# A selective-scan stage that reads its state out four tokens at a time, from channels that are neighbours in DRAM

## The chip, the cores and the metric

One core of one Trainium2 chip runs the whole program. The metric is device microseconds of one execution: the median of three executions for the kernel before, and one more execution with the hardware profiler, whose trace is read below. TensorE is called PE in the rows, its weight loads PEld, VectorE DVE, ScalarE ACT, GpSimd POOL, SyncE SP.

## The reference, cut to what matters

The program is a stack of eight blocks on 2048 tokens of 128 features (8 sequences of 256 tokens). The change touches one of them, a bidirectional Mamba block: two selective scans, m = 1 over each sequence and m = 2 over the reversed one, with 256 channels (E) and 64 states (N) a channel.

```
def step(h, inp):
    xt, dtt, Bt, Ct = inp
    dA = jnp.exp(dtt[:, :, None] * A)
    h = dA * h + (dtt * xt)[:, :, None] * Bt[:, None, :]
    y = jnp.einsum('ben,bn->be', h, Ct)
    return (h, y)
...
y = ys.transpose(1, 0, 2) + xc * Dp
y = y * _silu(z)
```

For every token the state h (256 channels x 64 states) is decayed, a term is added, and it is contracted with the 64 values of C of that token.

## The kernel before, in words

`mamba_scan` runs once for m = 1 and once for m = 2. A partition holds one state of one half of the channels: 64 states x 2 halves (g = 0, 1) = 128 partitions. The free axis holds 4 channels x 256 tokens. One **iteration** handles these 4 channels of each half for one sequence; 32 iterations (`NS`, 4 units u of 8 iterations i) make one sequence, tb; 8 sequences make one scan stage. So each stage has 256 iterations, and both stages 512. A sequence is one turn of a hardware loop on PE, ACT, DVE and POOL (the first is written out before the loop); SP's program is written out in full.

An iteration n goes through five queues, each in its own order:

- SP loads dt * x of the 4 channels, the same for all 64 states: two DMAs (`load_dtx`, one for each half of 64 partitions, 256 KB each) into one of 4 buffers `kept` (they lie in the memories `residual` and `norm`). It waits until POOL has finished product n - 4. `load_rows` brings the step sizes dt as bf16 rows, for PE.
- POOL multiplies with B (`times_b`, L3550) into one of 4 buffers `dBx`; it waits for the load of n and for scan n - 4.
- PE spreads dt over the 64 states (`cast`, L3436, two products, banks 0 and 1). Each half waits until ACT has read that bank in iteration n - 1.
- ACT takes the exponential (`exps`, L3492, four instructions) into one of 2 PSUM buffers `decay`; it waits for scan n - 2.
- DVE runs the recurrence as one scan instruction over 1024 elements (L3572) into `h`, which has 2 halves of 32 channels, one for each unit in turn.

The contraction with C comes after: `chunk` on PE (L3449), 9 iterations behind the cast. C stands on the weight side. `c_spread` holds, for each token, a tile of 16 columns that is zero but for the two columns (one for each half g) of that token, so 8 tokens that follow one another can be accumulated into 16 rows of PSUM. Four such groups of tokens go to PSUM partitions 0, 32, 64 and 96. A chunk covers 32 tokens of the 32 channels of a unit with 32 products of 16 columns by 32 channels. Each product stands in the trace as two PE records and two PEld records, as every f32 product does. At the end of a unit ACT copies the bank to `y_tokens` (`move`, L3511). Once a sequence, in iteration 11 of the next, `by_features` multiplies with the diagonal D (L3456) and turns `y_tokens` back with the identity (L3460), DVE multiplies with the gate (`gate`). At the start of a sequence ACT fills `c_spread` from C (`build`, L3504); its zeros come from DRAM by one DMA at the start of each stage (L3417).

Of the kernel before, what the change touches and what calls it, by code (L numbers as in the profile page):

```python
# [13 lines left out]
BF16 = mybir.dt.bfloat16  # L14
# [5 lines left out]
P = 128  # L20
# [2907 lines left out]
def lay_out_mamba(i, d, np):  # L2928
# [19 lines left out]
    d["l3a_zero"] = np.zeros(T * 16, np.float32)  # L2948
# [414 lines left out]
def mamba_scan(k, m, mem):  # L3363
# [5 lines left out]
    TALL = 16  # L3369
# [3 lines left out]
    with Part(k) as p:  # L3373
        h = p.sb("h", [P, 2, SJ, T])
        spread = p.sb("c_spread", [P, T, TALL])
        extra = p.sb("dBx", [P, 2, SSTEP])
        rows = p.sb("dt_rows", [SROWS, 2, 2, T], BF16)
        ysb = p.sb("y_tokens", [P, NI, P])
# [13 lines left out]
        state = lambda n, x: (2 * n + x // 2) * 8 + x % 2  # L3392
        by_token = lambda g: k.bank[YBANK].rearrange("p (n g s) -> p n g s", g=SE, s=8)[:, :, g, :]
        in_eights = lambda a: a.rearrange("p (n s) -> p n s", s=8)

        def tokens(tb, lo=0, n=T):
            return bass.ds(tb * T + lo, n)

        with nc.Block() as block:
            @block.sync  # L3400
            def _(sp):
                def load_rows(u):
                    tb, jb = u // SUNITS, u % SUNITS
                    sp.wait_ge(q["cast"], 2 * NI * u + 2 * NI)
                    sp.dma_start(rows[:, u % 2], mem["dt_rows"][:, 2 * jb:2 * jb + 2, tb * T:(tb + 1) * T]).then_inc(rows_in[u % 2], 16)

                def load_dtx(n):
                    tb, jb, i = n // NS, n // NI % SUNITS, n % NI
# [8 lines left out]
                sp.dma_start(spread[:].rearrange("p t c -> p (t c)"), k.dram["l3a_zero"].partition_broadcast(P)).then_inc(q["spread_zeroed"], 16)  # L3417
# [9 lines left out]
            def _(pe):  # L3427
                def cast(tb, l):
                    n, u, i = tb * NS + l, l // NI, l % NI
                    if i == 0:  # L3430
                        pe.wait_ge(rows_in[u % 2], 16 * (tb * (SUNITS // 2) + u // 2 + 1))
                    for x in range(2):
                        pe.wait_ge(q["decayed"], 2 * n + x + 1)
                        out = k.bank[x].rearrange("p (j t) -> p j t", t=T)[:, :, 1:]
                        a = 2 * i + x
# [272 lines left out]
```

## Time and profile before

| | |
|---|---|
| median of three executions | 5022.83 us (5010.32 to 5029.96) |
| profiled execution | 5026.35 us |
| its span, first to last instruction | 5024.5 us |
| granted TensorE clock, mean over the span | 0.831 |
| PE busy in the span | 3553.1 us (71%) |
| DVE busy | 3276.9 us (65%) |
| POOL busy | 2511.8 us (50%) |
| ACT busy | 2346.7 us (47%) |
| the two scan stages, first to last scan | about 3029 to 3902 us and 4042 to 4902 us |

A scan stage is found by the lines L3572 and L3550. Rows of idle time name what ended it: `issue` means that the engine waited for nothing that the profile shows. `PEclk` is the granted TensorE clock as a share of 2.4 GHz.

### The profile page before, as it was taken

The numbers are of one execution on the slowest core, as the hardware profiler recorded it, in microseconds if no ns is written. First come the engines' busy times: TensorE is split into PE (matmuls) and PEld (weight loads), VectorE is DVE, ScalarE is ACT, GpSimd is POOL, SyncE is SP. The second block draws the span as 40 slices with busy tenths as digits, with TensorE's granted clock in tenths as the row PEclk, the third lists the DMA queues.
The fourth block names the chain that finished last, engine by engine and source line by source line (L and its number), as shares of the span: only waits on it lengthen the run. The fifth ranks groups of instructions, "written<-read, shape, count | busy, mean of one in ns | idle before, by whom it ended". The sixth has DMA issues, their size and how long they took to land. (4 is left out here: it accounts for less than half of the span.)

```text
span 5024.5 us, 130170 instructions
## 1 busy us (share of the span) xinstructions
PE 3553.1 (71%) x50301; PEld 2406.5 (48%) x50301; DVE 3276.9 (65%) x5840; ACT 2346.7 (47%) x5437; POOL 2511.8 (50%) x2256
## 2 busy tenths in 40 slices
PE   5888888888488688688899744565656545556564
PEld 3666666666366466474477412333333323333333
DVE  5777777776476576562388666566667556666675
ACT  3555555555244344233366554444445444444451
POOL 2555555555343342430133426666667066666772
PEclk8999999999777778788999866777778867777787
DMA  1000000000000000000000028767777187776860
GB/s 49 8 9 9 9 9 9 9 8 8 15 0 6 13 0 6 5 0 24 17 1 0 14 78 184 154 154 165 153 161 163 47 183 159 158 155 156 164 159 31
DMA packets 263394, 333.14 MB, mean 66 GB/s; under 512 B 97056, under 2 KB 127024, under 8 KB 260912
## 3 DMA queue, kind: packets, MB, share of 16 engines
q1 hardware_dynamic: 262832, 325.11, 29.2%
q8 instruction: 418, 6.85, 0.6%
q14 instruction: 144, 1.18, 0.1%
HBM read 306.12 MB, written 18.87 MB: 65 GB/s over the span
## 5 line engine op out<-in xcount | busy, mean ns | idle before, releaser
L3492 ACT ACTIVATE banks<-banks,alog 128x255 f32<-128x255 f32 x2048 | 787.8, 447 | 864.2 <-PE banks L3436 796.8
L3449 PE MATMUL banks<-h,c_spread 128*16 128x32 f32 x32768 | 614.6, 234 | 550.0 <-issue 543.7
L3449 PEld LDWEIGHTS banks<-h,c_spread 128*16 128x16 f32 x32768 | 493.1, 115 | 856.1 <-issue 829.9
L3572 DVE TENSOR_TENSOR_SCAN h<-banks,dBx 128x1024 f32<-128x1024 f32 x256 | 576.0, 2279 | 392.5 <-ACT banks L3492 328.7
L3550 POOL TENSOR_TENSOR dBx<-residual,b_by_state 128x1024 f32<-128x1024 f32 x256 | 601.3, 2362 | 356.4 <-DVE h L3572 293.0
L3572 DVE TENSOR_TENSOR_SCAN h<-banks,norm_featmajor 128x1024 f32<-128x1024 f32 x256 | 576.4, 2277 | 226.2 <-ACT banks L3492 213.8
L3550 POOL TENSOR_TENSOR norm_featmajor<-norm,b_by_state 128x1024 f32<-128x1024 f32 x256 | 601.7, 2361 | 215.5 <-DVE h L3572 161.3
L3436 PE MATMUL banks<-dt_rows,selectors 96*128 96x510 bf16 x1024 | 446.7, 506 | 280.7 <-issue 126.3
L3436 PEld LDWEIGHTS banks<-dt_rows,selectors 96*128 96x128 bf16 x1024 | 87.3, 103 | 392.9 <-issue 212.8
L973 POOL TENSOR_TENSOR weighted<-probs,f 128x1024 f32<-128x1024 f32 x64 | 120.7, 1902 | 215.5 <-DVE f L1024 214.3
L2611 POOL TENSOR_TENSOR out_factors<-out_norms,exponents 128x4 f32<-128x4 f32 x64 | 64.4, 1007 | 288.9 <-DVE out_norms L2776 288.9
L2667 DVE SCALAR_TENSOR_TENSOR qk<-banks,taps,qk 128x255 f32<-128x255 f32 (+2 forms) x384 | 167.2, 477 | 26.6 <-ACT qk L2405 15.1
L2667 DVE SCALAR_TENSOR_TENSOR v_featmajor<-banks,taps,v_featmajor 128x255 f32<-128x255 f32 (+2 forms) x384 | 167.2, 477 | 24.4 <-ACT v_featmajor L2405 13.8
L1766 POOL TENSOR_TENSOR squares<-qkv_ahead 128x1024 f32<-128x1024 f32 x32 | 60.9, 1903 | 197.4 <-ACT qkv_ahead L1702 197.4
L2587 POOL TENSOR_TENSOR blocks_inv<-blocks_inv,block_products 64x14 f32<-64x14 f32 (+6 forms) x448 | 117.1, 261 | 63.8 <-issue 0.3
L2585 POOL TENSOR_TENSOR block_products<-blocks_inv,blocks 64x14 f32<-64x14 f32 (+6 forms) x448 | 114.0, 254 | 67.1 <-issue 5.5
L1595 PE MATMUL banks<-wqkv,x_batch 128*128 128x512 f32 x192 | 120.7, 779 | 26.9 <-DVEq L1792 23.8
L1211 POOL TENSOR_TENSOR norms<-norms,minus_half 128x64 f32<-128x64 f32 x8 | 84.7, 10592 | 106.0 <-DVE norms L1242 106.0
L159 POOL MEMSET minus_half<- 128x4 f32 x7 | 0.7, 102 | 270.3 <-POOLq L365 162.9
L255 PE MATMUL banks<-ident,norm 128*128 128x128 f32 x112 | 31.2, 435 | 135.9 <-ACT norm L230 134.1
L2475 ACT ACTIVATE v<-banks,beta_k 128x128 f32<-128x128 f32 x256 | 73.0, 368 | 100.0 <-PE banks L2255 100.0
L2405 ACT ACTIVATE qk<-banks,taps 128x256 f32<-128x256 f32 x128 | 53.6, 470 | 139.3 <-PE banks L2125 139.2
(451 smaller groups left out, 8768.8 us busy)
## 6 DMA issues: line engine op xcount, KB each, us to landing
residual<-mamba_dtx_rows SPq DMA_DIRECT2D x512, 256.0 KB, 5.8
norm<-mamba_dtx_rows SPq DMA_DIRECT2D x512, 256.0 KB, 6.3
dt_rows<-mamba_dt_rows SPq DMA_DIRECT2D x64, 96.0 KB, 7.0
delta_blocks<-A_turned SPq DMA_DIRECT2D x256, 8.0 KB, 1.5
inv_turned<-delta_blocks SPq DMA_DIRECT2D x256, 8.0 KB, 1.7
mamba_dtx_rows<-dtx SPq DMA_DIRECT2D x16, 256.0 KB, 2.3
c_spread<-in_l3a_zero SPq DMA_DIRECT2D x2, 2048.0 KB, 10.5
blocks<-delta_blocks SPq DMA_DIRECT2D x32, 64.0 KB, 2.1
```

Source lines behind the costliest of these rows:

```text
L973: nc.gpsimd.tensor_tensor(blocks(SW[:, u]), blocks(S[:, j % 2, u]), over(f[:, j % 2, 16 * u:16 * u + 16], T // NJ), ALU.mult).then_inc(wei ...
L1211: nc.gpsimd.tensor_tensor(nrm[:], nrm[:], half[:], ALU.pow).then_inc(norm_ready, 1)
L1595: i = nc.tensor.matmul(k.bank[4 + n][:], xb[:, t * P:(t + 1) * P], wqkv[:, n * 512:(n + 1) * 512], start=True, stop=True)
L2475: i = fn(v[:, hg, c, h, :], k.bank[c][:, h * P:(h + 1) * P], ACT.Identity, scale=sp[:, hg, c, h:h + 1])
L2585: tt(tmp[:, 0:j, 0:n], over(U[:, 0:j, j], n), across(N[:, j, j + 1:], j), ALU.mult)
L2587: i = tt(U[:, 0:j, j + 1:], U[:, 0:j, j + 1:], tmp[:, 0:j, 0:n], ALU.add)
L2667: i = stt(out=dst[:, back:], in0=k.bank[4 + n % 2][:, m * T:(m + 1) * T - back], scalar=taps[:, first + m, j:j + 1], in1=dst[:, back:], op ...
L3436: nc.tensor.matmul(out, mem["sel"][:, 2 * a:2 * a + 2, :].rearrange("r g n -> r (g n)"), rows[:, u % 2, :, 1:], start=True, stop=True).the ...
L3449: mm = nc.tensor.matmul(k.bank[OBANK][32 * c:32 * c + TALL, i * SJ:(i + 1) * SJ], spread[:, t, :], h[:, u % 2, :, t], start=s == 0, stop=s ...
L3492: e = fn(per_step(decay[l % 2])[:, 2 * x + j, 1:], k.bank[x][:, j * T + 1:(j + 1) * T], ACT.Exp, scale=mem["A"][:, at:at + 1])
L3550: nc.gpsimd.tensor_tensor(per_step(dBx[l % 4]), per_step(kept[l % 4]), across(mem["B"][:, tokens(tb)], 4), ALU.mult).then_inc(q["dbx"], 1)
L3572: v.tensor_tensor_scan(flat(h[:, u % 2, 4 * i:4 * i + 4, :]), decay[l % 2], dBx[l % 4], 0.0, ALU.mult, ALU.add).then_inc(q["scanned"], 1)
```

## The change

- **Four tokens in one product.** `c_spread` now has tiles of 32 columns for 4 tokens that follow one another (4 groups of 4 tokens, 2 halves). One product takes the states of those 4 tokens for all 32 channels as 128 moving columns. It computes every pair of the 4 tokens, and only the pairs with equal tokens are used. A chunk has 8 products of 32 by 128 in place of 32 of 16 by 32, and a unit's result fills all 512 columns of the bank in place of 256.
- **What follows from it.** `move` copies 512 columns in place of 256, and `y_tokens` is four times as large in its last axis; `by_features` turns it back with 16 products of 32 columns in place of 8 of 64. The zeros are 9280 bytes for a partition in place of 16384.
- **Neighbouring channels.** The 4 channels of an iteration were 2 + 2, 8 apart; now they are 4 in a row. A load reads one run of 4 KB for each partition in place of two of 2 KB, with the same bytes and the same two DMAs.
- **Rows of dt.** `load_rows` brings rows for two units at once (half as many DMAs, twice the size), and earlier: in iteration 4 of the 16 before, not in iteration 5 of the 8 before.

```
-    TALL = 16
+    NG, TALL, WIDE = 4, 32, 144
...
-        spread = p.sb("c_spread", [P, T, TALL])
+        spread = p.sb("c_spread", [P, NG * 4 * WIDE + 16])
-        ysb = p.sb("y_tokens", [P, NI, P])
+        ysb = p.sb("y_tokens", [P, NG, P, 4])
...
                 def load_dtx(n):
                     sp.wait_ge(q["dbx"], n + 1)
                     for g in range(SE):
-                        src = mem["dtx_rows"][tb, g].rearrange("(a r) t -> a r t", r=8)[2 * i:2 * i + 2, 2 * jb:2 * jb + 2, :]
-                        sp.dma_start(kept[n % 4][g * 64:(g + 1) * 64, :].rearrange("p (a x) -> p a x", a=2),
-                                     src.rearrange("a r t -> a (r t)").partition_broadcast(64)).then_inc(dtx_in[n % 4], 16)
+                        sp.dma_start(kept[n % 4][g * 64:(g + 1) * 64, :],
+                                     mem["dtx_rows"][tb, g, at:at + 4, :].rearrange("j t -> (j t)").partition_broadcast(64)).then_inc(dtx_in[n % 4], 16)
...
-                    if n % NI == 5 and n // NI + 1 < B * SUNITS:
-                        load_rows(n // NI + 1)
+                    if n == 2:
+                        load_rows(1)
+                    if n % (2 * NI) == 4 and 1 < n // (2 * NI) + 1 < 2 * B:
+                        load_rows(n // (2 * NI) + 1)
...
                 def chunk(tb, l):
-                    for s in range(8):
+                    part = i // 2
+                    out = k.bank[OBANK][:, part * P:(part + 1) * P].rearrange("p (j w) -> p j w", w=4)
+                    for quad in (2 * (i % 2), 2 * (i % 2) + 1):
                         for c in range(4):
-                            t = i * SJ + c * 8 + s
-                            mm = nc.tensor.matmul(k.bank[OBANK][32 * c:32 * c + TALL, i * SJ:(i + 1) * SJ], spread[:, t, :], h[:, u % 2, :, t],
-                                                  start=s == 0, stop=s == 7)
+                            t, at = part * 64 + c * 16 + quad * 4, (part * 4 + c) * WIDE + quad * TALL
+                            mm = nc.tensor.matmul(out[32 * c:32 * c + TALL], spread[:, at:at + TALL], h[:, u % 2, :, t:t + 4],
+                                                  start=quad == 0, stop=quad == 3)
...
-                    for i in range(NI):
-                        mm = nc.tensor.matmul(k.bank[YBANK][:, i * 64:(i + 1) * 64], ysb[:, i, :], used, start=False, stop=i == NI - 1)
+                    for n in range(NG):
+                        for w in range(4):
+                            mm = nc.tensor.matmul(out[:, n, :, :, :, w], ysb[:, n, :, w], ones[:, :, :, :, w], start=False,
+                                                  stop=n == NG - 1 and w == 3)
...
-                    out = ysb[:].rearrange("p n (a r) -> p n a r", r=8)[:, :, :, 2 * u:2 * u + 2]
-                    fn(out, k.bank[OBANK][:, 0:T].rearrange("p (n a r) -> p n a r", n=NI, r=2),
-                       ACT.Copy).then_inc(q["moved"], 1)
+                    out = ysb[:].rearrange("p n (x i v) w -> p n x i (v w)", x=2, i=NI)[:, :, u % 2, :, 16 * (u // 2):16 * (u // 2) + 16]
+                    fn(out, k.bank[OBANK].rearrange("p (n i v) -> p n i v", n=NG, v=16), ACT.Copy).then_inc(q["moved"], 1)
```

On PE, inside the loop over the sequences, one iteration stood like this before: two casts with the register work of their waits, then the 32 products of a chunk.

```order
L3433 ISA
L3436 MATMUL banks<-dt_rows,selectors 128x2x255
L3433 REGISTER_ALU
L3436 MATMUL banks<-dt_rows,selectors 128x2x255
L3449 MATMUL banks<-h,c_spread 16x32 x32
```

The same iteration of the changed kernel:

```order
L3434 ISA
L3436 MATMUL banks<-dt_rows,selectors 128x2x255
L3434 REGISTER_ALU
L3436 MATMUL banks<-dt_rows,selectors 128x2x255
L3451 MATMUL banks<-h,c_spread 32x128 x8
```

Nothing moved on PE; the row of 32 small products became one of 8 products with four times the columns.

On SP, iterations 8 to 29 of the first sequence before (`residual` and `norm` are the four `kept` buffers, two iterations each):

```order
L3405 DMA dt_rows<-mamba_dt_rows 96x2x256
L3412 DMA norm<-mamba_dtx_rows 64x2x512 x4
L3412 DMA residual<-mamba_dtx_rows 64x2x512 x4
L3412 DMA norm<-mamba_dtx_rows 64x2x512 x4
L3412 DMA residual<-mamba_dtx_rows 64x2x512 x4
L3405 DMA dt_rows<-mamba_dt_rows 96x2x256
```

The same queue of the changed kernel, about the load of rows that stands in iteration 20:

```order
L3410 DMA norm<-mamba_dtx_rows 64x1024 x4
L3410 DMA residual<-mamba_dtx_rows 64x1024 x2
L3404 DMA dt_rows<-mamba_dt_rows 96x4x256
L3410 DMA residual<-mamba_dtx_rows 64x1024 x2
L3410 DMA norm<-mamba_dtx_rows 64x1024 x4
```

The loads of dt * x kept their place and number, each with one run of 1024 elements in place of two of 512; the loads of rows stand half as often.

## Rows read from the trace of the kernel before

**Rows 1.** Stretches of both scan stages: length, busy us, clock, DMA share, GB/s.
```profile
core 0: us, PE busy (x) PEld busy (x) DVE busy (x) ACT busy (x) POOL busy (x), PEclk, DMA share, GB/s
3025.00:3930.00 905.00, 533.23 (x17108) 320.64 (x17109) 582.16 (x277) 416.53 (x1088) 597.21 (x255) 0.76 0.73 154
```

**Rows 2.** The scans alone (L3572), seven sequences of each stage.
```profile
3028.80:3809.40 780.60, 501.49 (x225) 0.74 0.76 160
4041.60:4813.30 771.70, 501.27 (x224) 0.75 0.76 162
```

**Rows 3.** Page, costliest groups: busy us, mean ns, idle before, releaser.
```profile
L3492 ACT ACTIVATE banks<-banks,alog 128x255 f32<-128x255 f32 x2048 | 787.8, 447 | 864.2 <-PE banks L3436 796.8
L3449 PE MATMUL banks<-h,c_spread 128*16 128x32 f32 x32768 | 614.6, 234 | 550.0 <-issue 543.7
L3572 DVE TENSOR_TENSOR_SCAN h<-banks,dBx 128x1024 f32<-128x1024 f32 x256 | 576.0, 2279 | 392.5 <-ACT banks L3492 328.7
L3550 POOL TENSOR_TENSOR dBx<-residual,b_by_state 128x1024 f32<-128x1024 f32 x256 | 601.3, 2362 | 356.4 <-DVE h L3572 293.0
```

**Rows 4.** PE in order of time, 3546 to 3588 us.
```profile
3546.87 0.51 PE L3449 MATMUL banks<-h,c_spread 128*16 128x32 f32 x23 [2.51 <-issue]
3547.32 1.03 PE L3436 MATMUL banks<-dt_rows,selectors 96*128 96x510 bf16 x2
3548.28 1.09 PE L3449 MATMUL banks<-h,c_spread 128*16 128x32 f32 x64
3549.31 1.03 PE L3436 MATMUL banks<-dt_rows,selectors 96*128 96x510 bf16 x2
3550.28 0.73 PE L3449 MATMUL banks<-h,c_spread 128*16 128x32 f32 x35
3553.51 0.63 PE L3449 MATMUL banks<-h,c_spread 128*16 128x32 f32 x29 [2.50 <-issue]
...
3586.69 1.03 PE L3436 MATMUL banks<-dt_rows,selectors 96*128 96x510 bf16 x2 [9.31 <-issue]
```

**Rows 5.** DMA packets by queue and kind, 3030 to 3930 us.
```profile
q8 instruction: 148, 2.42, 1.2%
```

**Rows 6.** DVE in order of time, the same stretch as rows 4.
```profile
3549.62 4.47 DVE L3572 TENSOR_TENSOR_SCAN h<-banks,norm_featmajor 128x1024 f32<-128x1024 f32 x2 [2.24 <-ACT banks L3492]
3589.00 2.29 DVE L3572 TENSOR_TENSOR_SCAN h<-banks,dBx 128x1024 f32<-128x1024 f32 x1 [9.38 <-ACT banks L3492]
```

**Rows 7.** POOL in order of time, start of stage m = 1, then of m = 2.
```profile
3026.60 2.34 POOL L3550 TENSOR_TENSOR dBx<-residual,b_by_state 128x1024 f32<-128x1024 f32 x1 [5.34 <-DMA residual<-mamba_dtx_rows]
...
3041.94 4.64 POOL L3550 TENSOR_TENSOR norm_featmajor<-norm,b_by_state 128x1024 f32<-128x1024 f32 x2 [2.08 <-DMA norm<-mamba_dtx_rows]
...
3063.20 2.34 POOL L3550 TENSOR_TENSOR norm_featmajor<-norm,b_by_state 128x1024 f32<-128x1024 f32 x1 [0.83 <-DMA norm<-mamba_dtx_rows]
...
4039.51 2.34 POOL L3550 TENSOR_TENSOR dBx<-residual,b_by_state 128x1024 f32<-128x1024 f32 x1 [5.40 <-DMA residual<-mamba_dtx_rows]
...
4075.72 2.34 POOL L3550 TENSOR_TENSOR dBx<-residual,b_by_state 128x1024 f32<-128x1024 f32 x1 [1.41 <-DMA residual<-mamba_dtx_rows]
```

**Rows 8.** Stretches at the starts of the stages, all engines, columns as in rows 1.
```profile
3023.00:3044.00 21.00, 9.22 (x16) 1.67 (x16) 13.30 (x6) 15.23 (x37) 13.68 (x6) 0.50 0.95 195
3044.00:3064.00 20.00, 10.61 (x311) 5.39 (x310) 17.56 (x8) 9.22 (x24) 17.43 (x9) 0.59 0.96 183
3017.00:3022.00 5.00, 0.00 (x0) 0.00 (x0) 0.00 (x0) 0.00 (x0) 2.34 (x1) 0.50 0.98 406
```

**Rows 9.** PE records of one line in a stretch, 32 columns (L3449).
```profile
3504.70:3505.90 1.20, 1.10 (x64) 0.50 0.66 148
```

**Rows 10.** The same for 128 columns (L3621), at both clocks.
```profile
3922.31:3924.31 2.00, 2.00 (x10) 0.55 0.00 0
3926.00:3931.00 5.00, 5.00 (x47) 1.00 0.00 0
```

**Rows 11.** PE in order of time at the end of stage m = 1.
```profile
3906.82 2.01 PE L3449 MATMUL banks<-h,c_spread 128*16 128x32 f32 x128 [1.22 <-issue]
3910.30 2.02 PE L3449 MATMUL banks<-h,c_spread 128*16 128x32 f32 x128 [1.46 <-issue]
3916.56 2.12 PE L3460 MATMUL banks<-ident,y_tokens 128*128 128x64 f32 x16
```

**Rows 12.** Groups, 2900 to 4900 us: copies of 256 and of 512 columns.
```profile
L3511 ACT ACTIVATE y_tokens<-banks 128x256 f32<-128x256 f32 x62 | 25.1, 405 | 55.8 <-PE banks L3449 55.4
L3218 ACT ACTIVATE dtx<-one_plus 128x512 f32<-128x512 f32 x16 | 9.2, 622 | 1.9 <-DVE one_plus L3297 1.8
```

More of the change, by code:

```diff
@@ L2947, in lay_out_mamba @@
     d["l3a_sel"] = np.concatenate([np.stack([e, z], 2), np.stack([z, e], 2)]).reshape(96, 32)
-    d["l3a_zero"] = np.zeros(T * 16, np.float32)
+    d["l3a_zero"] = np.zeros(16 * 144 + 16, np.float32)
 def load_mamba_weights(k, sp, mem, m):
@@ L3374, in mamba_scan @@
         h = p.sb("h", [P, 2, SJ, T])
-        spread = p.sb("c_spread", [P, T, TALL])
+        spread = p.sb("c_spread", [P, NG * 4 * WIDE + 16])
         extra = p.sb("dBx", [P, 2, SSTEP])
-        rows = p.sb("dt_rows", [SROWS, 2, 2, T], BF16)
-        ysb = p.sb("y_tokens", [P, NI, P])
+        rows = p.sb("dt_rows", [SROWS, 2, 4, T], BF16)
+        ysb = p.sb("y_tokens", [P, NG, P, 4])
         names = ("zeroed", "cast", "decayed", "dbx", "scanned", "chunked", "built", "moved", "y_ready", "y_read", "spread_zeroed",
@@ L3429, in cast @@
                     n, u, i = tb * NS + l, l // NI, l % NI
-                    if i == 0:
-                        pe.wait_ge(rows_in[u % 2], 16 * (tb * (SUNITS // 2) + u // 2 + 1))
+                    kh, row = u // 2, 8 * (u % 2) + i
+                    if u % 2 == 0 and i == 0:
+                        pe.wait_ge(rows_in[kh], 16 * (tb + 1))
                     for x in range(2):
@@ L3434, in cast @@
                         out = k.bank[x].rearrange("p (j t) -> p j t", t=T)[:, :, 1:]
-                        a = 2 * i + x
-                        nc.tensor.matmul(out, mem["sel"][:, 2 * a:2 * a + 2, :].rearrange("r g n -> r (g n)"),
-                                         rows[:, u % 2, :, 1:], start=True, stop=True).then_inc(q["cast"], 1)
+                        nc.tensor.matmul(out, mem["sel"][:, 2 * row:2 * row + 2, :].rearrange("r g n -> r (g n)"),
+                                         rows[:, kh, 2 * x:2 * x + 2, 1:], start=True, stop=True).then_inc(q["cast"], 1)
                 def chunk(tb, l):
@@ L3455, in by_features @@
                     for g in range(SE):
-                        nc.tensor.matmul(by_token(g), mem["diag"][:, g, :], in_eights(xc[:, g, tokens(tb)]), start=g == 0, stop=False)
+                        nc.tensor.matmul(by_token(g), mem["diag"][:, g, :], xc[:, g, tokens(tb)], start=g == 0, stop=False)
                     pe.wait_ge(q["moved"], tb * SUNITS + SUNITS + MOVES)
-                    used = k.ident[:].rearrange("p (c s) -> p c s", s=32)[:, :, 0:TALL]
-                    for i in range(NI):
-                        mm = nc.tensor.matmul(k.bank[YBANK][:, i * 64:(i + 1) * 64], ysb[:, i, :], used, start=False, stop=i == NI - 1)
+                    ones = k.ident[:].rearrange("p (c g a w) -> p g c a w", g=SE, a=4, w=4)
+                    out = k.bank[YBANK].rearrange("p (g n c a w) -> p n g c a w", g=SE, n=NG, a=4, w=4)
+                    for n in range(NG):
+                        for w in range(4):
+                            mm = nc.tensor.matmul(out[:, n, :, :, :, w], ysb[:, n, :, w], ones[:, :, :, :, w], start=False,
+                                                  stop=n == NG - 1 and w == 3)
                     mm.then_inc(q["y_ready"], 1)
@@ L3502, in build @@
                     lanes = slice(64 * g, 64 * g + 64)
-                    dst = spread[lanes, half * n:(half + 1) * n, :].rearrange("p (a s) c -> p a (s c)", s=8)[:, :, 8 * g:8 * g + 7 * 17 + 1:17]
-                    fn(dst, in_eights(mem["C"][lanes, tokens(tb, half * n, n)]), ACT.Copy).then_inc(q["built"], 1)
+                    lo = half * 8 * WIDE + 16 * g
+                    dst = spread[lanes, lo:lo + 8 * WIDE].rearrange("p (x a w) -> p x a w", a=4, w=36)[:, :, :, 0:4]
+                    src = mem["C"][lanes, tokens(tb, half * n, n)].rearrange("p (x a w) -> p x a w", a=4, w=4)
+                    fn(dst, src, ACT.Copy).then_inc(q["built"], 1)
                 def move(tb, u):
```

21 lines of the change are left out of this document (10 added, 11 removed).

## The prediction, made before the changed kernel ran

> **What bounds the kernel now.** The change lives in the two scan stages, so I read the stretch of one stage first [rows 1]: in 905 us no engine is busy for more than two thirds, so nothing computes all the time; something is waited for. The scans alone over seven sequences of each stage [rows 2] give the pace to be explained: 780.6 / 7 = 111.5 us a sequence for m = 1 and 771.7 / 7 = 110.2 us for m = 2, or 3.48 and 3.45 us an iteration of 32 in a sequence.
>
> The costliest groups [rows 3] give the chain of waits. DVE needs 2.28 us an iteration, POOL 2.36 us, ACT four instructions that run back to back. POOL mostly waits for DVE, DVE for ACT, ACT for PE's cast (796.8 us), and PE, the end of the chain, for `issue`: 543.7 us in which nothing in the profile was missing. PE in order of time [rows 4] shows what kind of idle time that is. It breaks off in the middle of a chunk, where no instruction waits for a semaphore: between two such breaks lie 23 + 2 + 64 + 2 + 35 = 126 matmul records, with their weight loads 252 instructions. A block of instructions of 16.4 KB (2.42 MB / 148) arrives 148 times in 900 us [rows 5]; the breaks are 6.6 us apart here and the blocks 900 / 148 = 6.1 us, so it is one break for each block, 65 B an instruction. PE runs dry because the next block of its own program is not there. The breaks of 2.5 us become gaps of 2.24 us on DVE, and the one of 9.31 us at the turn of the hardware loop becomes 9.38 us [rows 6]. Two buffers of `decay` do not cover them.
>
> The Trainium skill ("Runtime: NRT & Kernel Launch", Instruction fetch mechanics) states such 16 KiB blocks of 256 instructions, but calls the cost of crossing one mostly hidden. The trace shows the opposite here. By the page the change would give nothing through this door; by the rows it removes the wait.
>
> **What is bound next.** The first eight iterations of a stage have no chunk on PE, so they show the pace without these breaks. POOL starts iteration 1 at 3026.60 and iteration 14 at 3063.20 [rows 7]: 36.6 / 13 = 2.82 us. In stage m = 2 it is (4075.72 - 4039.51) / 12 = 3.02 us for iterations 1 to 13, a little of it waits for DVE. In both POOL waits again and again for the load of dt * x. The DMA engines are then 95% and 96% busy at 195 and 183 GB/s [rows 8], so this is a limit of throughput. An iteration loads 2 x 256 KB = 524 KB and 12 KB of rows, 537 KB; at the mean of 189 GB/s that is 2.84 us. The same engines moved 406 GB/s just before, when the zeros went to all 128 partitions [rows 8]: what is slow is the load to 64 partitions at a time, or its 2 KB runs.
>
> **The change, part by part.**
>
> *Fewer instructions on PE.* An iteration had 64 + 2 matmul records with their weight loads, 132 instructions; now it has 16 + 2, 36 instructions. A block lasts 252 / 36 = 7 iterations, about 20 us at 2.85 us each. From one break's end to the next in [rows 4] it was 6.6 us, and the break was 2.5 us of it, so a block arrives some 7 us after the one before it was begun. With 20 us there is room for even the longest (9.3 us). I take all breaks inside a sequence as gone. The turn of the loop may still stop PE for 9.3 us. Loads go on meanwhile: 9.3 / 2.85 = 3.3 iterations, which the 4 buffers `kept` and 4 `dBx` hold, and DVE catches up at 2.28 against 2.85 us. I leave 1.5 us a sequence for what is not caught up.
>
> *Cost of the wider products.* Not shown before in this form; bounds from both sides. 64 records of 32 columns took 1.10 us at half clock [rows 9]. A record of 128 columns takes 5.00 / 47 = 106 ns at full clock and 2.00 / 10 = 200 ns at about half [rows 10]; so 32 columns one after another at half clock would be 50 ns each, 3.2 us in all. The four column groups therefore ran together, with a gain of 2.9. 16 records of 128 columns are the same number of columns: with the same overlap 16 x 200 / 2.9 = 1.10 us at half clock and 0.6 us at full; without any overlap 3.2 us at half clock. I take 1.1 us, because the four groups are addressed as before. With two casts at 1.03 us [rows 4] PE needs 2.1 us an iteration, below 2.85 us: on PE nothing is bound. Cover that is needed: 0.75 us.
>
> *Turning back.* 16 products in place of 8: 16 records took 2.12 us [rows 11], and the time is nearer to that of the weight load than of the 64 columns, so 32 records take up to 4.2 us, 2.1 us more a sequence, once, in iteration 11. Behind it on PE is the cast of iteration 12. DVE has one or two decayed buffers by then (2.3 to 4.6 us), so a gap of 1 to 2 us on DVE is possible; POOL's products and the loads run on behind it, and it is part of the 1.5 us above.
>
> *ACT.* Four `move` a sequence grow from 0.41 to at most 0.62 us [rows 12], 0.9 us a sequence on an engine that is idle for more than half of the stage [rows 1]. Nothing on the path. The builds write the same elements: nothing.
>
> *The loads.* The same bytes in half as many runs. Above: I know no row for 4 KB runs to 64 partitions. Lower bound of what it brings: nothing, 2.84 us stay. Upper bound: the engines do 406 GB/s as with the zeros, 1.3 us, and POOL is bound at 2.36 us. I take 2.85 us, nearest to the row with the same 64 partitions. The rows of dt come earlier and half as often: PE waits of this kind are small and sit in the same gaps; nothing further.
>
> The Trainium skill ("SBUF — State Buffer", Door 1: The DMA port swizzle) speaks against a gain from the longer runs: the rate depends on how many of 16 ports the partitions reach, and a half of 64 partitions reaches eight. An estimate from its 436 GB/s is 218 GB/s, which would be 2.46 us an iteration whatever the run length. The rows show 183 to 195 GB/s, under that mark, so they fit it. By the page's figure the sum would be about 4520 us.
>
> *Start and end.* The zeros shrink from 2.1 to 1.2 MB: at 406 GB/s 2 us less before the first scan, two stages, 4 us. After the last scan of a stage the eight chunks of the last unit stand alone; two chunks then take 3.48 us (3906.82 to 3910.30) [rows 11], so eight 13.9 us. They become 8 x 0.6 to 8 x 1.1 us, so 5 to 9 us less each; with the longer turn back (2.1 us) I take 5 us, two stages, 10 us.
>
> **The sum.** A sequence becomes 32 x 2.85 + 1.5 = 92.7 us. Saved: 8 x (111.5 - 92.7) + 8 x (110.2 - 92.7) = 150 + 140 = 290 us, and 14 us at the starts and ends: 304 us. The profiled execution took 5026.35 us, 3.5 us above the median of the runs shown; so 4722 us for it and 4718 us for a median.
>
> **The rivals.**
>
> *The longer runs, or a better mix of the two halves in the DMA engines, lift the rate, and POOL is bound.* For it: the mean rate over a stage is 160 GB/s at 76% busy engines [rows 2], which is 211 GB/s at 100%, more than at the starts. Against it: 195 and 183 GB/s at 95% [rows 8]. POOL at 2.36 us gives 32 x 2.36 + 1.5 = 77.0 us a sequence: 16 x (110.85 - 77.0) + 14 = 556 us less, 4467 us. At 211 GB/s it is 2.54 us, 82.8 us a sequence and 4560 us. I see this case mostly between 4460 and 4640 us.
>
> *The turn of the loop is not absorbed.* If every queue has to refetch its program at the turn, or loads stop too, the 9.3 us stay whole: 100.5 us a sequence, 16 x (110.85 - 100.5) + 14 = 180 us less, 4843 us. For it: a gap of that size stands on DVE [rows 6]. Against it: the buffers ahead of DVE.
>
> *The column groups do not run together with 128 columns.* One mechanism that ends slower: 16 records at 200 ns in sequence and the casts make 3.2 + 1.03 = 4.2 us an iteration, 135 us a sequence, 16 x 24 = 390 us more, 5400 us. It decides from about 3.45 us an iteration on PE, that is from 2.4 us a chunk. Against it: [rows 9] at half clock; and a PE so busy should be granted the full clock, where 16 x 106 ns = 1.7 us and the loss vanishes.
>
> *The breaks have nothing to do with the number of instructions.* Then the pace of a sequence stays, and only the ends gain: about 5010 us. Against it: the count of 252 between them.
>
> **How the numbers follow.** DMA bound near 2.85 us: 0.57, its own range 4640 to 4800 us. Faster loads: 0.22. The turn of the loop kept: 0.14. Slower: 0.04. Unchanged: 0.03. The range for 8 in 10 takes the first case, about half of the second and most of the third: 4540 to 4870 us. A measurement of this kernel tells about 0.5%, 25 us, from no change. Faster 0.94, same 0.03, slower 0.03.
>
> **What would show it.** Right: PE's idle time before the chunk's line with `issue` falls from 550 us to under 150 us; POOL's waits end with the loads and no longer with DVE; DMA share in a stage 0.9 or more at 180 to 200 GB/s; scans 2.85 us apart; a chunk of 16 records in 0.6 to 1.1 us. Wrong: a chunk over 2.4 us; POOL without idle time (loads faster); gaps of 9 us on DVE every 32 scans that the pace behind them does not make up; DMA busy below 80%.

## Result and the profile after

| | before | after |
|---|---|---|
| median of 4 runs, us | 5021.14 (5010.32 to 5029.96) | 4516.3 (4507.34 to 4525.06) |
| ratio | | 0.8995, interval 0.8968 to 0.9023 |
| a sequence, stage m = 1 and m = 2, us | 111.5 and 110.2 | 78.6 and 77.6 |

The saving is 505 us where I had forecast 304; 4516 us lies below the range of 4540 to 4870. The profiled execution took 4510.49 us. Of all executions below, one of turning_spread stood apart (5531 us, at a mean granted clock of 0.54) and is left out. First the scans of each stage alone, as in [rows 2]; columns: length, DVE busy (instructions), clock, DMA share, GB/s.

```profile
3005.40:3555.40 550.00, 493.42 (x224) 0.63 0.88 220
3768.70:4312.10 543.40, 493.74 (x225) 0.63 0.88 222
```

550.0 / 7 = 78.6 us. At [rows 2] the same bytes took 780.6 us at 160 GB/s. The costliest groups of the page, to be read against [rows 3]:

```profile
L3497 ACT ACTIVATE banks<-banks,alog 128x255 f32<-128x255 f32 x2048 | 788.5, 448 | 410.3 <-DVE h L3578 257.5
L3578 DVE TENSOR_TENSOR_SCAN h<-banks,dBx 128x1024 f32<-128x1024 f32 x256 | 572.6, 2267 | 145.0 <-ACT banks L3497 139.9
L3556 POOL TENSOR_TENSOR dBx<-residual,b_by_state 128x1024 f32<-128x1024 f32 x256 | 597.2, 2353 | 101.2 <-DVE h L3578 57.7
L3451 PE MATMUL banks<-h,c_spread 128*32 128x128 f32 x8192 | 488.4, 381 | 14.5 <-DVE h L3578 9.8
```

PE's idle time before the chunk is 14.5 us and none of it is `issue`, where it was some 550 us. ACT now waits for DVE (257.5 us) more than for PE's cast (148.3 us), where it was nearly all PE's cast. PE in order of time, over the end of one sequence and the start of the next (the rows down to 3515 us, beside [rows 4]) and at the end of the stage (beside [rows 11]):

```profile
3499.66 2.08 PE L3458 MATMUL banks<-xc,diagonal_d 128*128 x4
3501.53 7.47 PE L3464 MATMUL banks<-ident,y_tokens 128*128 128x32 f32 x32
3508.81 1.04 PE L3436 MATMUL banks<-dt_rows,selectors 96*128 96x510 bf16 x2
3509.78 1.08 PE L3451 MATMUL banks<-h,c_spread 128*32 128x128 f32 x16
...
3515.44 0.64 PE L3451 MATMUL banks<-h,c_spread 128*32 128x128 f32 x16
...
3634.31 5.71 PE L3451 MATMUL banks<-h,c_spread 128*32 128x128 f32 x128 [3.49 <-DVE h L3578]
...
3640.93 7.50 PE L3464 MATMUL banks<-ident,y_tokens 128*128 128x32 f32 x32
```

A chunk takes 1.08 us at the lower level of the clock and 0.64 us at the full one. Turning back takes 7.47 us. What that does to DVE (beside [rows 6]) and to POOL (beside [rows 7]), each in order of time; in brackets the idle time before the row:

```profile
3498.50 4.44 DVE L3578 TENSOR_TENSOR_SCAN h<-banks,norm_featmajor 128x1024 f32<-128x1024 f32 x2
...
3511.12 4.47 DVE L3578 TENSOR_TENSOR_SCAN h<-banks,dBx 128x1024 f32<-128x1024 f32 x2 [8.18 <-ACT banks L3497]
...
3648.47 0.76 DVE L3585 TENSOR_TENSOR silu_z<-banks,silu_z 128x256 f32<-128x256 f32 x2 [14.21 <-PE banks L3464]
```

```profile
3434.84 4.66 POOL L3556 TENSOR_TENSOR dBx<-residual,b_by_state 128x1024 f32<-128x1024 f32 x2 [4.81 <-DVE h L3578]
```

Last a stretch of 310 us inside stage m = 1, all engines (PE, PEld, DVE, ACT, POOL), and POOL's two groups over 3160 to 3600 us:

```profile
3250.00:3560.00 310.00, 273.43 (x2408) 127.25 (x2412) 277.28 (x135) 206.40 (x536) 290.83 (x127) 0.65 0.89 218
```

```profile
L3556 POOL TENSOR_TENSOR dBx<-residual,b_by_state 128x1024 f32<-128x1024 f32 x90 | 209.8, 2351 | 27.1 <-DVE h L3578 27.1
L3556 POOL TENSOR_TENSOR norm_featmajor<-norm,b_by_state 128x1024 f32<-128x1024 f32 x90 | 209.8, 2351 | 0.0
```

POOL is busy for 290.8 of 310 us, and over 3160 to 3600 us it waits for no load. In both stages together it waits for loads for 45.8 us, 39 us of it before the first two products of each stage. It is the bound: an iteration costs its 2.31 us, and once a sequence it stops, for 4.8 us in most sequences, behind the 7.5 us of turning back. 32 x 2.31 + 4.8 = 78.7 us, which is the pace measured in stage m = 1; in m = 2 some of the stops are shorter. DMA carries 218 GB/s at a share of 0.89 and is not waited for. What it moved in 40 slices of 9 us each, 3240 to 3600 us:

```profile
GB/s 241 238 233 227 112 234 231 230 225 236 236 234 175 164 235 236 231 227 239 227 230 120 222 234 236 229 228 237 233 229 111 234 234 228 220 249 236 225 223 106
```

The slices near 110 and 170 are those in which POOL stands still behind the turning back: no buffer `kept` comes free, and SP's loads wait for one.

The rest of the account: the stretches from the first scan of a stage to its last fell from 874.6 to 628.9 us and from 860.7 to 621.2 us, 485 us together. Each start (from DVE's clearing of the bank to the first scan) fell by some 2.5 us (from 19.1 to 16.8 us in m = 1), and the ends fell by 1.1 and 1.9 us: 493 us. The two profiled executions differ by 516 us; of the other 23 us some 21 lie before the first stage, in parts that the change doesn't touch, and first scans of other kernels here stand anywhere between 3000 and 3028 us.

### The profile page after: what moved, and what is told of

It reads as the page before. It is cut to its first block and busy times, and to the rows that moved or that the text cites. A ratio compares the mean times of both kernels' runs of the same rounds, so it can differ in the third digit from the quotient of the medians.

```text
span 4508.6 us, 81480 instructions
## 1 busy us (share of the span) xinstructions
PE 3596.5 (80%) x25981; PEld 2276.0 (50%) x25981; DVE 3262.1 (72%) x5840; ACT 2357.1 (52%) x5437; POOL 2497.6 (55%) x2256
## 5 line engine op out<-in xcount | busy, mean ns | idle before, releaser
L3497 ACT ACTIVATE banks<-banks,alog 128x255 f32<-128x255 f32 x2048 | 788.5, 448 | 410.3 <-DVE h L3578 257.5
L3436 PE MATMUL banks<-dt_rows,selectors 96*128 96x510 bf16 x1024 | 544.7, 544 | 250.5 <-ACT banks L3497 151.4
L3556 POOL TENSOR_TENSOR dBx<-residual,b_by_state 128x1024 f32<-128x1024 f32 x256 | 597.2, 2353 | 101.2 <-DVE h L3578 57.7
L3451 PE MATMUL banks<-h,c_spread 128*32 128x128 f32 x8192 | 488.4, 381 | 14.5 <-DVE h L3578 9.8
L3436 PEld LDWEIGHTS banks<-dt_rows,selectors 96*128 96x128 bf16 x1024 | 105.9, 105 | 639.7 <-ACT banks L3497 544.4
L3451 PEld LDWEIGHTS banks<-h,c_spread 128*32 128x32 f32 x8192 | 278.1, 145 | 223.1 <-issue 171.0
L1595 PE MATMUL banks<-wqkv,x_batch 128*128 128x512 f32 x192 | 105.2, 690 | 27.0 <-DVEq L1792 23.9
```

What stands on the lines that cost most here:

```text
L1595: i = nc.tensor.matmul(k.bank[4 + n][:], xb[:, t * P:(t + 1) * P], wqkv[:, n * 512:(n + 1) * 512], start=True, stop=True)
L3436: nc.tensor.matmul(out, mem["sel"][:, 2 * row:2 * row + 2, :].rearrange("r g n -> r (g n)"), rows[:, kh, 2 * x:2 * x + 2, 1:], start=True, ...
L3451: mm = nc.tensor.matmul(out[32 * c:32 * c + TALL], spread[:, at:at + TALL], h[:, u % 2, :, t:t + 4], start=quad == 0, stop=quad == 3)
L3497: e = fn(per_step(decay[l % 2])[:, 2 * x + j, 1:], k.bank[x][:, j * T + 1:(j + 1) * T], ACT.Exp, scale=mem["A"][:, at:at + 1])
L3556: nc.gpsimd.tensor_tensor(per_step(dBx[l % 4]), per_step(kept[l % 4]), across(mem["B"][:, tokens(tb)], 4), ALU.mult).then_inc(q["dbx"], 1)
```

## Experiments

Columns of the summary are the median in us and the ratio to the kernel before, measured beside it on the same chip (5021 to 5028 us there).

| run | us | ratio (interval) |
|---|---|---|
| old_places | 4773.2 | 0.9511 (0.9476 to 0.9546) |
| new_loads_only | 4684.7 | 0.9337 (0.9305 to 0.9369) |
| two_runs_near | 4521.1 | 0.9003 (0.8975 to 0.9030) |
| four_apart | 4515.7 | 0.8986 (0.8947 to 0.9024) |
| six_apart | 4519.0 | 0.8992 (0.8953 to 0.9031) |
| seven_apart | 4777.1 | 0.9520 (0.9408 to 0.9631) |
| nine_apart | 4789.2 | 0.9538 (0.9466 to 0.9610) |
| sixteen_apart | 4797.5 | 0.9546 (0.9505 to 0.9587) |
| halves_same | 4516.4 | 0.8987 (0.8948 to 0.9025) |
| far_by_dma | 4832.5 | 0.9630 (0.9504 to 0.9756) |
| two_a_turn | 4546.4 | 0.9042 (0.8995 to 0.9089) |
| quarter_of_c | 4492.0 | one run |
| half_of_c | 4499.0 | one run |
| turning_spread | 4475.0 | 0.8906 (0.8872 to 0.8941) |

**Products without loads, loads without products.** old_places is the kernel after with the loads of the kernel before:

```diff
-                        sp.dma_start(kept[n % 4][g * 64:(g + 1) * 64, :],
-                                     mem["dtx_rows"][tb, g, at:at + 4, :]...
+                        src = mem["dtx_rows"][tb, g].rearrange("(a r) t -> a r t", r=8)[2 * i:2 * i + 2, 2 * jb:2 * jb + 2, :]
+                        sp.dma_start(kept[n % 4][g * 64:(g + 1) * 64, :].rearrange("p (a x) -> p a x", a=2), ...
```

> The changed kernel, but each load of dt * x reads two runs of 2 KB that lie 8 channels apart, as before the change; everything else is as changed, so the state of most channels is fed with dt * x of other channels. Theory of the runs (the loads became faster because one run of 4 KB stands for two of 2 KB): the loads are back at about 189 GB/s, 2.84 us an iteration, POOL waits for them again, a sequence takes about 92 us, the whole 4720 us, which is what I predicted for the change itself. Rival (the loads were slow before only beside PE's stalls and its instruction blocks, or at the start of a stage): the time stays at 4516 us within 15 us and the DMA engines move 210 GB/s or more in a stage.

new_loads_only is the kernel before with the loads of the kernel after:

```diff
+                    at = 32 * jb + 4 * i
-                        src = mem["dtx_rows"][tb, g].rearrange("(a r) t -> a r t", r=8)[2 * i:2 * i + 2, 2 * jb:2 * jb + 2, :]
+                        sp.dma_start(kept[n % 4][g * 64:(g + 1) * 64, :],
+                                     mem["dtx_rows"][tb, g, at:at + 4, :].rearrange("j t -> (j t)")...
```

> The kernel before with one thing of the change: each load of dt * x reads one run of 4 KB of neighbouring channels (most channels are then fed with dt * x of others). Theory (PE's instruction blocks bound the kernel before): PE still stops every 252 instructions, the pace of a sequence hardly moves, 4960 to 5020 us. Rival (a block waits in the queues of the DMA engines behind the data, so cheaper data brings the blocks sooner): 4 to 6 us a sequence and more off, under 4930 us, with the number of the stops as before and each one shorter.

Everything but the places of the loads (called the products here) saves 248 us alone, the loads save 336 us alone, both 505 us. That is less than the sum of 584; that each relieves a chain in which the other waits too is my reading of it. In old_places no block of instructions comes for PE over the stretch below either, so fewer instructions end the breaks whatever the loads do. old_places is near the time that I had forecast for the whole change, at 94.9 us a sequence where I had 92.7. Its scans alone (columns as above), a stretch of all engines, and POOL's group over 3150 to 3600 us:

```profile
3005.90:3670.20 664.30, 508.10 (x225) 0.57 0.89 182
...
3250.00:3560.00 310.00, 243.71 (x2043) 107.59 (x2046) 243.94 (x115) 174.63 (x453) 246.99 (x107) 0.59 0.84 183
```

```profile
L3557 POOL TENSOR_TENSOR dBx<-residual,b_by_state 128x1024 f32<-128x1024 f32 x78 | 182.5, 2345 | 52.3 <-DMA residual<-mamba_dtx_rows 48.6 <-DVE h L3579 3.6
```

POOL waits 48.6 us for the buffers in `residual` (38.1 us for those in `norm`), against nothing in the kernel after. 183 GB/s against 218: the old loads cost the difference. new_loads_only shows that PE's breaks get shorter when the data loads are cheaper. PE in order of time there:

```profile
3421.40 0.52 PE L3449 MATMUL banks<-h,c_spread 128*16 128x32 f32 x23 [1.98 <-issue]
...
3451.07 1.03 PE L3436 MATMUL banks<-dt_rows,selectors 96*128 96x510 bf16 x2 [5.42 <-issue]
```

The breaks are still there, with the old number of blocks a turn (67 in 310 us, 19 a sequence of 87.8 us), but shorter. Over six turns of each kernel they are 91 before with 3.0 us on average and 9.3 us the longest, and 87 here with 1.7 us and 6.0 us. A block's own transfer did not get shorter: 114 blocks before, at 1.2% of 16 engines over 679 us, make 1.1 us each, and the 67 here, at 1.7% over 310 us, make 1.3 us. So the time was lost before the transfer. That the blocks stood behind data fits this, but no run shows it directly.

**Run length or place.** two_runs_near keeps runs of 2 KB, with their starts 3 KB apart (the scans then read other channels, same sizes):

```diff
-                                     mem["dtx_rows"][tb, g, at:at + 4, :]...
+                        lo = min(at, 122)
+                        src = mem["dtx_rows"][tb, g, lo:lo + 6, :].rearrange("(a r) t -> a r t", r=3)[:, 0:2, :]
```

> The changed kernel, but each load reads two runs of 2 KB with 1 KB between them (some channels are fed with dt * x of a neighbour). It parts run length from place. If the length of a run sets the rate, this is as slow as the two runs 8 channels apart (about 4720 us if the theory of the runs holds). If the distance in DRAM sets it, this is as fast as the change, 4516 us. If neither kernel is slower than the change, the loads have nothing to do with it.

It runs at 4521 us, as the kernel after does, and a load lands in 4.4 to 4.5 us as there (4.4), at the same 218 GB/s. Run length is worth nothing here; the distance of the two runs is. The next five kernels put another number D for 3 (rows `lo:lo + 2 * D`, `r=D`), so that the starts lie D KB apart: 9, 4, 6, 16 and then 7.

> The changed kernel, but each load reads two runs of 2 KB whose starts lie 9 KB apart in DRAM (in the slow form it was 8 KB, in the fast one 3 KB; some channels are fed with dt * x of others). If two places with the same offset within 8 KB (or another power of two) get in each other's way: fast, 4520 us. If distance as such costs: slow, about 4770 us.

> The changed kernel with two runs of 2 KB whose starts lie 4 KB apart (some channels fed with dt * x of others). 3 KB apart was fast (4521 us), 8 and 9 KB were slow (4773 and 4789 us). If the cost comes with distance little by little: about 4560 us. If it comes at a boundary between 3 and 8 KB: either 4520 or about 4770 us.

> As the run with 4 KB, with 6 KB between the starts. Little by little: about 4650 us. At a boundary: 4520 or about 4770 us.

> As the run with 4 KB, with 16 KB between the starts. If two places more than 8 KB apart are all alike: about 4770 to 4790 us. If the cost grows with distance: over 4850 us.

> The changed kernel with two runs of 2 KB whose starts lie 7 KB apart (some channels fed with dt * x of others). 6 KB apart was fast (4519 us), 8 KB slow (4773 us). If only a distance of 8 KB and more is slow: 4520 us. If the ends of the two runs together may not span more than 8 KB (7 KB apart they span 9 KB): about 4770 us.

The stretch 3250 to 3560 us of six_apart and of seven_apart:

```profile
3250.00:3560.00 310.00, 275.47 (x2429) 127.79 (x2428) 278.98 (x136) 206.80 (x538) 292.44 (x127) 0.65 0.88 219
```

```profile
3250.00:3560.00 310.00, 242.45 (x2033) 107.49 (x2033) 242.56 (x115) 174.40 (x452) 244.72 (x106) 0.58 0.89 181
```

A step, not a slope: up to 6 KB (both runs within 8 KB) 4516 to 4521 us, from 7 KB on (9 KB) 4773 to 4797 us. It is not a matter of powers of two, since 4 is fast and 7 and 9 are slow. As all runs are 2 KB, the distance of the starts (6 or 7 KB) and the span of both (8 or 9 KB) can't be told apart. The fast ones are not at a limit of the loads: 218 GB/s is what POOL asks for. Two more runs ask what the distance belongs to. In halves_same both halves of the partitions read the same 4 KB, where the kernel after has them 128 KB apart:

```diff
-                                     mem["dtx_rows"][tb, g, at:at + 4, :]...
+                                     mem["dtx_rows"][tb, 0, at:at + 4, :]...
```

> The changed kernel, but both halves load the same 4 KB of an iteration (channels of half 1 are fed with dt * x of half 0), where they were 128 KB apart. If the number of places in DRAM that are read at one time sets the rate, the DMA engines move more than the 243 GB/s that they have at full load in the changed kernel, and each load lands sooner than in 4.4 us; the time stays near 4516 us, since POOL and PE bound it. If the 64 partitions at a time set what is left, the rate at full load stays at 243 GB/s.

In far_by_dma each run of 2 KB is a DMA of its own, and the starts of the two of a half lie 8 KB apart:

```diff
-                        sp.dma_start(kept[n % 4][g * 64:(g + 1) * 64, :], ...
+                        for half in range(2):
+                            lo = min(at, 116) + 8 * half
+                            sp.dma_start(kept[n % 4][g * 64:(g + 1) * 64, half * 512:(half + 1) * 512],
+                                         mem["dtx_rows"][tb, g, lo:lo + 2, :]...
...
-                    pool.wait_ge(dtx_in[l % 4], 32 * (tb * (NS // 4) + l // 4 + 1))
+                    pool.wait_ge(dtx_in[l % 4], 64 * (tb * (NS // 4) + l // 4 + 1))
```

> The changed kernel with four DMAs an iteration in place of two: each brings one run of 2 KB to 64 partitions, and the two of a half read 8 KB apart (some channels fed with dt * x of others). If it is the places as such that cost, the packets are as slow as in the run with old places (a twentieth of them over 340 ns) and a sequence takes 93 us or more. If it is the turn from one place to the other inside one DMA, the packets are as fast as with two runs near each other (a twentieth over 170 ns); SP then needs four issues of about 0.6 us an iteration, 2.4 us, so a sequence takes 79 to 84 us, 4530 to 4600 us.

halves_same gains nothing (4516.4 us). POOL bounds both kernels, so the time alone says little; but a load lands in 4.3 us against 4.4, and the slices reach 248 GB/s against 249, so the 128 KB between the halves cost next to nothing. far_by_dma is slow (4832 us). Its queue in the stretch, columns packets, MB, share of the engines:

```profile
q1 hardware_dynamic: 35242, 54.56, 93.1%
```

At a share of 93% it moves 54.56 MB in 310 us, 176 GB/s, so two runs of 2 KB that start 8 KB apart are slow even when each is a DMA of its own. How much of its 4832 us comes from having four DMAs an iteration in place of two stays open, since four DMAs with near runs were not run. Packets of 2 KB show it from the other side: over the same stretch their median is 133 ns in two_runs_near with 5% over 171 ns, 129 ns in old_places with 5% over 291 ns, and 172 ns in far_by_dma with 5% over 333 ns; the shortest is 81 ns in all. Some packets are held up, and not all alike. What holds them no run here tells.

**The loop of PE.** In the kernel after no block of instructions comes for PE over 3160 to 3600 us (the last one of stage m = 1 before its end comes in the first turn of the loop, at 3149 us), and no gap with `issue` stands at the turn of the loop, which I had not forecast at all. A turn of it has some 1220 matmul and weight-load instructions. two_a_turn writes two sequences into one turn:

```diff
-                with pe.Fori(1, B) as tb:
-                    body(tb, False)
+                body(1, False)
+                with pe.Fori(1, B // 2) as pair:
+                    body(pair * 2, False)
+                    body(pair * 2 + 1, False)
```

> The changed kernel with PE's loop written for two sequences a turn (three turns in place of seven); only PE's program is longer, its work and order are the same. In the changed kernel a turn of PE's loop has about 1220 matmul and weight-load instructions and no block of instructions is fetched in a stage; before, a turn had about 4280 and 17 blocks. Theory (PE keeps the body of a loop that is small enough, and the change made it small enough): at 2450 a turn the body may no longer fit; then 9 to 10 blocks a turn are fetched again, hidden inside a sequence (4 to 5 blocks in 78 us), but the turn itself stops PE for 5 to 9 us, three times a stage, 20 to 60 us in all, 4530 to 4580 us. Rival (no limit between 1220 and 2450, or fewer instructions an iteration are all that counts): 4516 us within 15 us and no blocks.

quarter_of_c and half_of_c are the kernel before with the new loads and 12, or 16, of its 32 products with C an iteration; the rest of each sum over C is left out. The edit of quarter_of_c beside new_loads_only (half_of_c has 4 and 3 in place of 3 and 2):

```diff
-                    for s in range(8):
+                    for s in range(3):
...
-                                                  start=s == 0, stop=s == 7)
+                                                  start=s == 0, stop=s == 2)
```

> The kernel before with the new loads (one run of 4 KB) and 12 of the 32 small products of each chunk; the others are left out, so most tokens miss their sum over C. A turn of PE's loop has about 1700 matmul and weight-load instructions in place of 4280. If the body of a loop stays in PE when it is small enough, and the limit lies above this: no blocks in a stage, no stops at the turn, a sequence of 74 to 79 us, about 4450 to 4520 us. If only the pace of the instructions counts: 7 blocks a sequence, no stop inside it, but 5 to 9 us at each turn, 4530 to 4600 us.

> As the run with 12 products, with 16 of 32 in each chunk: about 2220 instructions a turn. If a limit lies between 1700 and 2220: 9 blocks a sequence, each hidden or nearly so, and stops of 5 to 9 us at each turn, 4530 to 4600 us. If the limit lies above: as with 12 products.

PE's blocks in 310 us (packets, MB, share), of two_a_turn, quarter_of_c and half_of_c in this order:

```profile
q8 instruction: 23, 0.38, 0.6%
```

```profile
q8 instruction: 37, 0.61, 0.9%
```

```profile
q8 instruction: 43, 0.70, 1.1%
```

| kernel | matmul and load instructions a turn | blocks a turn | instructions / 252 |
|---|---|---|---|
| before | 4264 | 19 | 16.9 |
| two_a_turn | 2448 | 11.6 | 9.7 |
| half_of_c | 2216 | 11 | 8.8 |
| quarter_of_c | 1704 | 9 | 6.8 |
| after | 1224 | 0 | 4.9 |

A loop of 1700 such instructions is fetched anew each turn, with about two blocks more than it fills; one of 1220 is not fetched again. quarter_of_c and half_of_c have the old, short turning back, so POOL is busy for 303.14 of 310 us in quarter_of_c and the time of its one execution is below that of the kernel after. Over 3160 to 3600 us its PE waits 27.2 us for instructions in six places, 5.3 us at most, all at the turn, and nearly all of it is covered. The limit lies between (other instructions of PE, waits above all, come on top and were not counted). In two_a_turn PE stands still for 4.5 and 4.9 us at the two turns in that window, and DVE for 3.6 us behind the first. It costs 30 us (4546 against 4516), with intervals that overlap a little; in the profiled executions the two stages, from first scan to last, are 19.5 us longer than in the kernel after, and the rest lies outside them. So a loop that is not fetched again is worth 20 to 30 us here; the fetch itself, once short, is mostly covered.

**Turning back, spread out.** turning_spread has the kernel after's 16 turning products over the iterations 10 to 15 of the next sequence, 2, 3, 3, 3, 3 and 2, where they stood together in one:

```diff
-                        if l == NI + 3 and not first:
-                            by_features(tb - 1)
+                        if l in turned and not first:
+                            by_features(tb - 1, turned[l])
...
+                turned = {10: range(0, 2), 11: range(2, 5), 12: range(5, 8), 13: range(8, 11), 14: range(11, 14), 15: range(14, 16)}
```

> The changed kernel with its 16 turning products spread over iterations 10 to 15 (2, 3, 3, 3, 3, 2) in place of all in iteration 11. In the changed kernel DVE stands for 8.2 us behind them once a sequence, and POOL for 4.8 us. Theory (the stall is the burst that the two decayed buffers cannot cover): the stall shrinks below what POOL can absorb, POOL runs without idle time at 2.31 us an iteration, a sequence takes 74 to 75 us, 16 x 4 to 4.8 us less, 4440 to 4455 us. Rival (the work is only moved; at half clock casts, chunk and three turning products need 3.5 us an iteration, above 2.2 us, so DVE loses the same sum in small pieces): 4490 to 4516 us.

4475.0 us, the best of all, and better than the kernel after by more than the intervals (0.8906 against 0.8995), at 532.9 / 7 = 76.1 us a sequence. That lies between the theory (4440 to 4455 us) and its rival (4490 to 4516 us): it gained 41 us by the medians, and 35 us in the two stages of the profiled execution. The theory took a stop of 4 to 4.8 us for each of 16 sequences; the page's row of POOL above has 57.7 us in all, so no spreading could gain more than that. PE, then DVE, then the stretch in which the products lie:

```profile
3426.33 1.04 PE L3436 MATMUL banks<-dt_rows,selectors 96*128 96x510 bf16 x2
3427.30 1.08 PE L3451 MATMUL banks<-h,c_spread 128*32 128x128 f32 x16
3428.31 1.61 PE L3465 MATMUL banks<-ident,y_tokens 128*128 128x32 f32 x6
```

```profile
3428.55 2.29 DVE L3581 TENSOR_TENSOR_SCAN h<-banks,norm_featmajor 128x1024 f32<-128x1024 f32 x1 [1.56 <-ACT banks L3500]
...
3432.04 2.29 DVE L3581 TENSOR_TENSOR_SCAN h<-banks,dBx 128x1024 f32<-128x1024 f32 x1 [1.20 <-ACT banks L3500]
```

```profile
3423.50:3445.00 21.50, 21.50 (x153) 13.40 (x145) 14.95 (x7) 10.43 (x29) 18.87 (x10) 0.50 0.79 218
```

The three rows of PE make 1.04 + 1.08 + 1.61 = 3.7 us an iteration, above POOL's 2.31 us, so gaps of up to 1.6 us on DVE stand in the place of one of 8.2. PE is busy for all 21.5 us, at a granted clock of 0.50 (1.2 GHz). The work was moved, not made less, and the smaller gaps are covered in part: POOL waits for DVE for 10.6 us over 3160 to 3600 us, where it was 27.1. An estimate for more iterations, at one product each (1.61 / 3 = 0.54 us), is 2.7 us on PE, still above POOL's 2.31; that was not tried.

## Why the prediction was right and where it failed

**Right: breaks, chunk, move, start.** The breaks inside a sequence were those of PE's own instructions; they are gone with the instructions. A chunk takes 1.08 and 0.64 us where I had 1.1 and 0.6: the four column groups overlap with 128 columns as they did with 32. The `move` takes 605 ns of the 0.62 us allowed. A start gains 2.3 us of the 2 that I had. The rival of serial column groups is out. My argument there that so busy a PE should be granted the full clock was wrong: the stage now has 273.4 of 310 us busy at 0.65, where [rows 1] had 533 of 905 us at 0.76, and the 21.5 us without a pause in turning_spread stand at 0.50.

**The failing step: the loads.** I wrote "I take 2.85 us, nearest to the row with the same 64 partitions". The loads after carry 218 GB/s at 0.89, in most slices of 9 us 220 to 249 GB/s, and inside the stage POOL waits for none. The rival "faster loads, POOL bound" came true. My reading of [rows 8] as a limit of throughput was right for the old loads, and old_places (94.9 us a sequence against my 92.7, 4773 us against my 4718) shows that the rest of the sum nearly stood. What failed was to carry the 2.85 us over to loads from other places: that row mixed the 64 partitions, the 2 KB runs and the places of the two runs in DRAM, 8 KB apart, and of the last two only the places count. The bound from above was in my text, and only its chance, 0.22, was too small. My words for the rival, "longer runs", were wrong too: two_runs_near has the old length and the new rate.

The Trainium skill ("SBUF — State Buffer", Door 1: The DMA port swizzle) gave me an estimate of 218 GB/s for loads to 64 partitions and some 4520 us, which is near the time measured. The trace agrees in the result and not in the reason: slices of 9 us reach 249 GB/s, and quarter_of_c carries 228 GB/s over 310 us, both above the estimate; what keeps the time at 4516 us is POOL, which waits for no load. In the kernel before, its 183 to 195 GB/s were not "under that mark, so they fit" but held down by another cause.

**Mis-sized: turning back.** I had up to 4.2 us for 32 records, from the 2.12 us of 16. Measured are 7.47 us, 233 ns a record, and 2.08 us for the diagonal ahead of them. The stretches of the 16 records of [rows 11] in the kernel before and of the 32 after, all engines:

```profile
3916.56:3918.68 2.12, 2.00 (x17) 1.83 (x15) 0.00 (x0) 0.00 (x0) 0.00 (x0) 1.00 0.00 0
```

```profile
3501.53:3509.00 7.47, 7.47 (x34) 7.41 (x33) 1.41 (x1) 0.00 (x0) 7.25 (x4) 0.73 0.84 227
```

The row that I priced it from stood at the full clock, with most of its records 112 ns apart. After, they are 233 ns apart from the first to the last, and in turning_spread, where the clock is 0.50 throughout, 233 ns as well. So 233 ns is the price at the lower level, and the clock was what I had left out; that the row for 7.47 us gives 0.73 and not 0.50 stays unexplained. PEld is busy for 7.41 of the 7.47 us, so it is the weight loads that take the time, as I had it.

The gap on DVE is 8.18 us where I had 1 to 2. It makes up to 4.8 us of a sequence on POOL, 57.7 us in both stages, and the 1.5 us left for it were too few. Against the faster loads it went the other way. The rival's 77.0 us a sequence was 1.6 us short of the measured 78.6: 3.3 us from this stop, less 32 x 0.05 = 1.6 us because a product on POOL costs 2.31 us and not 2.36. The ends of the stages gained 1.1 and 1.9 us, not 5 each: eight chunks take 5.71 us as forecast, but the longer turn back takes 7.50 us behind them.

**Wrong, and harmless: the turn of the loop.** I had it stay at 9.3 us, absorbed. There is none. The Trainium skill ("Runtime: NRT & Kernel Launch", Instruction fetch mechanics) has block crossings mostly hidden. At [rows 4] they cost 2.5 to 9.3 us. With 1700 to 2450 instructions a turn and the new loads there are few breaks inside a turn and one of 3.7 to 5.4 us at its end, much of it covered; so the trace comes nearer to the rule with fewer instructions and cheaper loads. It also adds to my cause: in the kernel before the blocks were late in part because the data loads were slow (3.0 us a break, 1.7 in new_loads_only).

The rest of the difference, 505 against 304 us: old_places to after is 257 us, the loads. What is left, the products alone, is 248 us measured, to my 304 us. Of the 56 us between them some 34 are the pace (16 sequences of 94.9 us where I had 92.7) and some 7 the ends of the stages.

## What to carry to other kernels

When a load runs under the best rate seen, list everything in which it differs from the fast one (partitions, run length, distance of its runs in DRAM), and don't give the rate to the one you know of; here neighbours in DRAM were worth 257 us. A sequence of single waits on `issue` at even counts of instructions is an engine out of instructions: fewer instructions cured it here, lighter data loads shortened it, and a loop short enough wasn't fetched again at all. Work that is moved into one place once a turn (here 16 products, 32 records, of which each waits for its 128 x 128 weights) is to be priced by its weight loads at the lower level of the clock, and spread over iterations with room.

## What was not expected of the hardware

- Two runs of 2 KB, broadcast to 64 partitions each, carry at least the 218 GB/s that POOL asks for when both lie within 8 KB of DRAM, and 181 to 183 GB/s when they span 9 KB or more (176 GB/s as two DMAs); the 128 KB between the loads of the two halves cost next to nothing (a load lands in 4.4 us, and in 4.3 us without them). The cause is open.
- A loop on PE of some 1220 matmul and weight-load instructions was not fetched again after its first turn; one of some 1700 was, wholly, in 9 blocks a turn.
- PE's breaks for instructions are longer when data loads are slow: they shrank from 3.0 to 1.7 us on average, and the longest from 9.3 to 6.0 us, by the change of the loads alone.
- The same turning-back records stood 112 ns apart at the full clock and 233 ns apart at the lower level.
- PE was busy without a pause for 21.5 us of turning products and casts, and the granted clock of that stretch was 0.50.
